# New orders of the steps in the attention loops of a four-layer transformer on one core

## The chip, the cores and the metric

The kernel runs on one core of a Trainium2 chip. The metric is the device time of one execution in microseconds. The core has five engines that each work through a queue of their own, strictly in the order in which the program put the instructions: TensorE (PE), VectorE (DVE), ScalarE (ACT), GpSimd (POOL) and SyncE (SP, here for DMAs alone). They meet only through semaphores.

## What is computed

Eight sequences of 256 tokens, width 128, pass through four layers. Each layer is a gated cross attention on a context of 64 tokens and a gated feed-forward block (mixtures of experts in layers 0, 1 and 3, a plain gated one in layer 2). Cut to the attention:

```
x = x + tanh(g_xattn[L]) * attn_L(layernorm(x), ctx)     # x: (8, 256, 128), ctx: (8, 64, 128)
x = x + tanh(g_ffn[L])   * ffn_L(layernorm(x))           # for L = 0..3

attn_0, attn_2:  16 heads of 8, keys and values from ctx; attn_2 adds a mask before the softmax
attn_1:          16 heads of 8, keys and values from ctx and from x itself (64 + 256 keys),
                 the first key gets tanh(gate), a layernorm follows before the output projection
attn_3:          8 heads of 64, keys and values from ctx
```

## The kernel before

Everything stays in SBUF; the program is a row of stages (`setup`, then attention and feed-forward of each layer, then `store`). The change lies in `attention` (layers 0, 1, 2) and `attention3` (layer 3).

An attention stage has a prologue (weights split into high and low parts, the keys of all sequences) and a loop over the eight sequences b. The work of one sequence is cut into steps, for 16-head layers by group g of four heads (g = 0 to 3), in layer 1 also by the set of keys i (i = 0 the context's, i = 1 to 4 one head's own). On the engines, a step is this:

- `scale` (DVE L804, layer 3 L1181): normalises x into `xn`. `turn`: PE transposes `xn` (L518, L1035), ACT and DVE split the result into `xt_hi` and `xt_lo` (L686, L810), POOL adds the output bias to x (L394, L987).
- `proj` (g): PE multiplies with the weights (L535 to L537) into the one bank `b_proj`; ACT takes a part (L698), DVE makes `q` from the bank and the part (L823). PE's next `proj` waits for that (`qk_split`), since the bank is the same. In layer 3 the two `proj` (L1044 to L1046) are copied by ACT (L1137).
- `keys` (g): POOL spreads this sequence's keys into `kc` (L398). It waits until the last sequence's `weights` of this group have read it.
- `scores` (g): PE multiplies `q` and `kc` (L551, mask L553; own keys L558; layer 3 L1057); it waits for `q` and `kc`. DVE reduces to a maximum (L835, L837, L1192) and puts it in `mx` (L847, L849, L1197).
- `maxima` (g): PE transposes the maxima (L571, L1064), ACT and DVE split them (L705, L858, L860; layer 3 L1142, L1203).
- `weights` (g): PE computes the scores again, transposed and less their maximum (L586, L588, L590, L591, L597, layer 3 L1073 and L1074); ACT takes the exponential (L711, L1147).
- `values` and `spread`: POOL lays out the values (L405, L1008), and in layer 1 those of x itself. `pv`: PE multiplies with them (L624, L1092), ACT copies the result (L725). Layer 3 also has `sums` (PE L1081, DVE reciprocal L1208), `parts` (ACT L1152, DVE L1213) and `divide` (PE L1100, ACT copy L1157, DVE L1220).
- `o_turn`, `o_norm`, `o_scale`, `on_turn`, `y`: the result is transposed back (L641), divided (L865, L868), in layer 1 normalised (POOL L465, DVE L888), transposed (L647), projected (L653, L1114) and added to x (L895, L1226).
- `mask_in`, `mask` (layer 2): POOL copies this sequence's mask (L458), PE transposes it (L526), ACT and DVE split it (L692, L817), POOL keeps a copy (L453). `scores` waits for the DVE's part.

The order of the steps is written out by hand in one table for each layer, `STEPS_0` to `STEPS_3`. An entry names a step, an offset to the pass number v, and the group. Each engine goes over the same table and issues its own part of each step, so a table sets the order of four queues at once:

```
def passes(eng, does):
    for v in range(-2, B + 3):
        for step, db, *at in table:
            if step in does and 0 <= v + db < B:
                does[step](v + db, *at)
```

Work of up to three sequences is so interleaved. The offset and the place in the table together say how far a step stands behind another. Every wait is inside its step and moves with it.

Of the kernel before, what the change touches and what calls it, by code (L numbers as in the profile page):

```python
# [113 lines left out]
def setup(pr):  # L114
# [2176 lines left out]
```

## Time and profile before

| | us |
|---|---|
| median of 3 runs | 1176.37 |
| the three runs | 1165.46, 1176.37, 1176.54 |
| the profiled execution | 1168.41 |
| its span (first to last instruction) | 1166.6 |

| loop over the eight sequences | first `scale` starts | last `y` on DVE starts |
|---|---|---|
| layer 0 | 35.6 | 125.6 |
| layer 1 | 208.2 | 442.2 |
| layer 2 | 747.5 | 861.8 |
| layer 3 | 943.7 | 1069.7 |

Over the whole span PE is busy for 78%, DVE 64%, ACT 48%, POOL 37%; but these are means over stages with different limits, so the loops are read one by one. A matmul's time in the profile runs to its modelled end, while the next may start some 0.12 us after it; PE's idle time is therefore read from starts.

### The profile page before, as it was taken

What the parts mean: (1) busy time and instruction counts of PE and PEld (TensorE: products, weight loads), DVE (VectorE), ACT (ScalarE), POOL (GpSimd) and SP (SyncE); (2) the same over time, 40 slices, a digit from 0 to 9 for tenths busy, and PEclk for the clock granted to TensorE, in tenths of its full rate; (3) what the DMA queues carried; (4) which work ended last, traced back from release to release, by engine and by line L of the source; (5) the groups of instructions that cost most, each with busy time, mean ns of one, the idle gap of its engine ahead of it and who ended that gap; (6) DMA issues with size and microseconds to landing.
All of it is one profiled execution on the core that took longest, in us unless ns stands there. A gap on an engine that the chain in (4) does not pass through costs nothing. (4 is left out here: it accounts for less than half of the span.)

```text
span 1166.6 us, 17099 instructions
## 1 busy us (share of the span) xinstructions
PE 912.0 (78%) x5366; PEld 686.6 (59%) x5366; DVE 746.8 (64%) x1823; ACT 563.8 (48%) x1091; POOL 428.7 (37%) x575
## 2 busy tenths in 40 slices
PE   2799586689899885888888885688858588885696
PEld 2677464556565643666666663477745357884574
DVE  3688467579998865757666564467756414555576
ACT  0477253367776762545555543256634233331364
POOL 2333414133443323655656565233310132220434
PEclk9799688689998995999999998689979769998699
DMA  4000000000001000000000001000000200000001
GB/s 129 1 2 2 1 0 22 1 20 20 19 21 37 20 2 0 1 1 1 1 1 1 1 1 23 16 2 1 2 21 1 72 1 1 1 1 1 0 1 37
DMA packets 25606, 14.12 MB, mean 12 GB/s; under 512 B 10775, under 2 KB 25006, under 8 KB 25390
## 3 DMA queue, kind: packets, MB, share of 16 engines
q1 hardware_dynamic: 25518, 13.03, 4.2%
q8 instruction: 45, 0.74, 0.3%
q14 instruction: 43, 0.35, 0.1%
HBM read 11.98 MB, written 1.05 MB: 11 GB/s over the span
## 5 line engine op out<-in xcount | busy, mean ns | idle before, releaser
L1433 POOL TENSOR_TENSOR L1f_h<-L1f_h,L1f_gb 128x512 f32<-128x512 f32 (+1 forms) x96 | 152.2, 1589 | 105.5 <-DVE L1f_h L1726 97.3
L711 ACT ACTIVATE L_pt<-bank 128x512 f32<-128x512 f32 x224 | 127.1, 597 | 44.0 <-PE bank L597 35.0
L398 POOL TENSOR_TENSOR L_kc<-L_kc_all,const 128x256 fp32r<-128x256 f32 x96 | 59.1, 618 | 177.8 <-PE bank L597 114.1
L698 ACT ACTIVATE L_part<-bank,L_bias_ca,const 128x256 fp32r<-128x256 f32 x128 | 68.9, 563 | 89.3 <-PE bank L537 88.8
L1562 ACT ACTIVATE L1f_a<-bank 128x512 f32<-128x512 f32 (+1 forms) x96 | 57.3, 597 | 112.7 <-PE bank L1487 112.6
L1726 DVE TENSOR_TENSOR L1f_h<-L1f_a,bank 128x512 f32<-128x512 f32 (+1 forms) x96 | 65.5, 682 | 70.8 <-ACT L1f_a L1562 70.3
L1734 DVE TENSOR_TENSOR L1f_h_lo<-L1f_h,L1f_h_hi 128x512 fp32r<-128x512 f32 (+1 forms) x96 | 88.2, 919 | 11.1 <-ACT L1f_h_hi L1575 11.1
L837 DVE TENSOR_REDUCE L_ms<-bank 128x2 f32<-128x512 f32 x128 | 84.0, 686 | 7.3 <-PE bank L558 7.2
L835 DVE TENSOR_REDUCE L_mc<-bank 128x8 f32<-128x512 f32 (+1 forms) x96 | 65.4, 682 | 19.5 <-PE bank L553 12.2
L1485 PE MATMUL bank<-L1f_xt_hi,big_hi 128*128 128x512 f32 (+1 forms) x192 | 77.8, 405 | 0.0
L1486 PE MATMUL bank<-L1f_xt_lo,big_hi 128*128 128x512 f32 (+1 forms) x192 | 76.8, 400 | 0.0
L1487 PE MATMUL bank<-L1f_xt_hi,big_lo 128*128 128x512 f32 (+1 forms) x192 | 76.7, 400 | 0.0
L558 PE MATMUL bank<-L_k,L_q 32*128 32x256 f32 x256 | 54.3, 335 | 16.6 <-DVE L_ms L837 15.1
L551 PE MATMUL bank<-L_kc,L_q 128*128 128x256 f32 x192 | 54.1, 345 | 15.8 <-DVE L_msk L817 6.4
L1507 PE MATMUL bank<-L1f_h_hi,big_hi 128*128 128x512 f32 (+1 forms) x96 | 41.4, 431 | 30.0 <-DVE L1f_h_lo L1734 29.7
L823 DVE SCALAR_TENSOR_TENSOR L_q<-bank,L_bias_c,L_part 128x256 fp32r<-128x256 f32 x96 | 46.2, 482 | 25.8 <-ACT L_part L698 23.6
L1575 ACT CAST L1f_h_hi<-L1f_h 128x512 fp32r<-128x512 f32 (+1 forms) x96 | 59.0, 615 | 2.1 <-POOL L1f_h L1433 2.1
L558 PEld LDWEIGHTS bank<-L_k,L_q 32*128 32x128 f32 x256 | 35.5, 199 | 32.9 <-DVE L_ms L837 21.3
L535 PE MATMUL bank<-L_xt_hi,L_wx 128*128 128x256 f32 x128 | 43.1, 337 | 9.9 <-DVE L_xt_lo L810 9.9
L551 PEld LDWEIGHTS bank<-L_kc,L_q 128*128 128x128 f32 x192 | 34.5, 208 | 27.6 <-issue 16.5
L705 ACT ACTIVATE L_hm<-bank,const 128x256 fp32r<-128x256 f32 x96 | 45.1, 470 | 6.3 <-PE bank L571 6.1
L1507 PEld LDWEIGHTS bank<-L1f_h_hi,big_hi 128*128 128x128 f32 (+1 forms) x96 | 17.9, 187 | 49.9 <-DVE L1f_h_lo L1734 44.8
(412 smaller groups left out, 2570.2 us busy)
## 6 DMA issues: line engine op xcount, KB each, us to landing
L_raw<-in_L_ffn_w_dram SPq DMA_DIRECT2D x8, 176.0 KB, 2.3
L_raw<-in_L_ffn_v_dram SPq DMA_DIRECT2D x8, 176.0 KB, 2.4
const<-in_const_dram SPq DMA_DIRECT2D x1, 1036.0 KB, 5.1
x<-in_x_dram SPq DMA_DIRECT2D x2, 512.0 KB
L_raw<-in_L_ffn_w_dram SPq DMA_DIRECT2D x8, 128.0 KB, 2.5
L_mask<-in_mask_Bx1xSxS_ff_dram SPq DMA_DIRECT2D x2, 512.0 KB
out_dram<-x SPq DMA_DIRECT2D x2, 512.0 KB
L_raw<-in_L_ffn_w_dram SPq DMA_DIRECT2D x8, 48.0 KB, 2.6
```

The source lines that it names most:

```text
L551: last = pe.matmul(o[:, t * S:(t + 1) * S], q[:, g, ts], kc[:, g], start=True, stop=not masked)
L558: last = pe.matmul(o[:, t * S:(t + 1) * S], q[rows, g, t * P:(t + 1) * P], k[rows, g], start=True, stop=True)
L698: last = act.activation(part[:, i].bitcast(F32R), b_proj[:, i * S:(i + 1) * S], ACT.Identity, bias=bias_ca[:, i, g:g + 1], scale=pr.c("ak" ...
L711: act.activation(pt[:, g // 2, (g % 2) * NS + (HEADS_1[i] if own_keys else i)], b_st[(g * NS + i) % 2][:], ACT.Exp, scale=scale).then_inc( ...
L835: dve.tensor_reduce(mc[:].rearrange("p t j -> p (t j)"), by_head[:, :, start:], AX_X, ALU.max).then_inc(sem["sc_taken"], 1)
L837: dve.tensor_reduce(ms[:, :, i - 1], bank.rearrange("p (t s) -> p t s", s=S), AX_X, ALU.max).then_inc(sem["sc_taken"], 1)
L1433: pool.tensor_tensor(h[0:m, r], h[0:m, r], gb[0:m, gate_slot(c)], ALU.mult).then_inc(sem["h_done"], 1)
L1485: pe.matmul(bank[0:m], hi[:, at:at + m], xh, start=True, stop=False)
L1486: pe.matmul(bank[0:m], hi[:, at:at + m], xl, start=False, stop=False)
L1487: last = pe.matmul(bank[0:m], lo[:, at:at + m], xh, start=False, stop=True)
L1726: dve.tensor_tensor(h[0:m, r], a[0:m, r], b_u[c % NS][0:m], ALU.mult).then_inc(sem["half_done"], 1)
L1734: dve.tensor_tensor(h_lo[0:m, r], h[0:m, r], h_hi[0:m, r].bitcast(F32), ALU.subtract).then_inc(sem["lo_done"], 1)
```

## The change

The four tables are replaced. The steps in each are the same ones, the bodies of the steps, their waits, the buffers and the prologues of the stages as well; what changes is the place and the offset of the entries, and so the order in the queues of PE, DVE, ACT and POOL. No DMA moves.

For layers 0 and 2, this is PE's queue over one turn of the loop. Digits are the groups, b is the sequence whose `turn` begins the row.

```
layer 0 before: turn(b) scores3(b-1) proj0(b) maxima2(b-1) weights1(b-1) o_turn(b-2) scores0(b) proj1(b)
  maxima3(b-1) weights2(b-1) pv0(b-1) on_turn(b-2) scores1(b) proj2(b) maxima0(b) weights3(b-1) y(b-2)
  scores2(b) proj3(b) maxima1(b) weights0(b) pv1(b-1)
layer 0 after:  turn(b) maxima1(b-1) weights0(b-1) scores3(b-1) pv1(b-2) proj0(b) maxima2(b-1)
  weights1(b-1) o_turn(b-2) proj1(b) maxima3(b-1) weights2(b-1) on_turn(b-2) scores0(b) proj2(b)
  pv0(b-1) scores1(b) y(b-2) maxima0(b) proj3(b) weights3(b-1) scores2(b)
layer 2 before: as layer 0 before, with mask(b) between weights1(b-1) and o_turn(b-2)
layer 2 after:  turn(b) weights0(b-1) scores3(b-1) maxima2(b-1) proj0(b) weights1(b-1) o_turn(b-2)
  mask(b) proj1(b) weights2(b-1) scores0(b) maxima3(b-1) on_turn(b-2) proj2(b) scores1(b) pv0(b-1)
  maxima0(b) weights3(b-1) y(b-2) scores2(b) proj3(b) maxima1(b) pv1(b-1)
layer 3 before: turn(b) pv0(b-1) sums(b-1) proj0(b) y(b-2) proj1(b) scores0(b) scores1(b) pv1(b-1)
  maxima(b) divide0(b-1) divide1(b-1) weights0(b) weights1(b)
layer 3 after:  turn(b) divide1(b-2) weights0(b-1) proj0(b) weights1(b-1) proj1(b) pv0(b-1) sums(b-1)
  scores0(b) scores1(b) y(b-2) maxima(b) divide0(b-1) pv1(b-1)
```

On POOL, `keys` moves against `turn` in all layers (in layer 1, `turn(b)` now stands ahead of `keys0(b)`); on DVE, `scale(b+1)` moves ahead, in layer 2 from behind `y(b-2)` to behind `proj1(b)`, in layer 0 to behind `maxima2(b-1)`. In layer 1 a few entries swap with their neighbours.

```diff
--- before.py
+++ after.py
@@ -172,40 +172,40 @@
 
 
 STEPS_0 = (
-    ("values", 0), ("scale", 1), ("scores", 0, 2, 0), ("proj", 0, 3), ("keys", 0, 3), ("maxima", 0, 1), ("weights", 0, 0, 0), ("pv", -1, 1, 0),
-    ("turn", 1), ("scores", 0, 3, 0), ("proj", 1, 0), ("keys", 1, 0), ("maxima", 0, 2), ("weights", 0, 1, 0), ("spread", 0), ("o_turn", -1),
-    ("o_norm", -1), ("scores", 1, 0, 0), ("proj", 1, 1), ("keys", 1, 1), ("maxima", 0, 3), ("weights", 0, 2, 0), ("pv", 0, 0, 0), ("o_scale", -1),
-    ("on_turn", -1), ("scores", 1, 1, 0), ("proj", 1, 2), ("keys", 1, 2), ("maxima", 1, 0), ("weights", 0, 3, 0), ("y", -1),
+    ("keys", 0, 0), ("o_scale", -2), ("weights", -1, 3, 0), ("scores", 0, 2, 0), ("turn", 1), ("maxima", 0, 1), ("weights", 0, 0, 0),
+    ("scores", 0, 3, 0), ("pv", -1, 1, 0), ("proj", 1, 0), ("keys", 0, 1), ("maxima", 0, 2), ("keys", 0, 2), ("weights", 0, 1, 0), ("scale", 2),
+    ("o_turn", -1), ("o_norm", -1), ("proj", 1, 1), ("keys", 0, 3), ("maxima", 0, 3), ("weights", 0, 2, 0), ("on_turn", -1), ("scores", 1, 0, 0),
+    ("proj", 1, 2), ("pv", 0, 0, 0), ("scores", 1, 1, 0), ("y", -1), ("maxima", 1, 0), ("proj", 1, 3), ("spread", 0), ("values", 1),
 )
 
 STEPS_1 = (
-    ("y", -2), ("weights", -1, 3, 3), ("keys", 0, 2), ("keys", 0, 3), ("weights", -1, 3, 4), ("scores", 0, 1, 4), ("scores", 0, 2, 0), ("scale", 1),
-    ("proj", 0, 3), ("values", 0), ("maxima", 0, 1), ("pv", -1, 1, 0), ("weights", 0, 0, 0), ("pv", -1, 1, 1), ("keys", 1, 0), ("scores", 0, 2, 1),
-    ("scores", 0, 2, 2), ("weights", 0, 0, 1), ("weights", 0, 0, 2), ("pv", -1, 1, 2), ("weights", 0, 0, 3), ("scores", 0, 2, 3),
-    ("weights", 0, 0, 4), ("scores", 0, 2, 4), ("turn", 1), ("weights", 0, 1, 0), ("scores", 0, 3, 0), ("scores", 0, 3, 1), ("maxima", 0, 2),
-    ("proj", 1, 0), ("spread", 0), ("pv", -1, 1, 3), ("pv", -1, 1, 4), ("scores", 0, 3, 2), ("weights", 0, 1, 1), ("weights", 0, 1, 2),
-    ("scores", 0, 3, 3), ("scores", 0, 3, 4), ("o_turn", -1), ("weights", 0, 1, 3), ("weights", 0, 1, 4), ("o_norm", -1), ("scores", 1, 0, 0),
-    ("proj", 1, 1), ("weights", 0, 2, 0), ("pv", 0, 0, 0), ("weights", 0, 2, 1), ("weights", 0, 2, 2), ("scores", 1, 0, 1), ("scores", 1, 0, 2),
-    ("maxima", 0, 3), ("pv", 0, 0, 1), ("pv", 0, 0, 2), ("weights", 0, 2, 3), ("scores", 1, 0, 3), ("o_scale", -1), ("weights", 0, 2, 4),
-    ("scores", 1, 0, 4), ("proj", 1, 2), ("keys", 1, 1), ("on_turn", -1), ("scores", 1, 1, 0), ("maxima", 1, 0), ("weights", 0, 3, 0),
-    ("pv", 0, 0, 3), ("pv", 0, 0, 4), ("scores", 1, 1, 1), ("weights", 0, 3, 1), ("weights", 0, 3, 2), ("scores", 1, 1, 2), ("scores", 1, 1, 3),
+    ("y", -2), ("weights", -1, 3, 3), ("weights", -1, 3, 4), ("scores", 0, 1, 4), ("scores", 0, 2, 0), ("scale", 1), ("proj", 0, 3), ("values", 0),
+    ("maxima", 0, 1), ("weights", 0, 0, 0), ("scores", 0, 2, 1), ("scores", 0, 2, 2), ("pv", -1, 1, 0), ("pv", -1, 1, 1), ("weights", 0, 0, 1),
+    ("weights", 0, 0, 2), ("pv", -1, 1, 2), ("weights", 0, 0, 3), ("scores", 0, 2, 3), ("weights", 0, 0, 4), ("scores", 0, 2, 4), ("turn", 1),
+    ("weights", 0, 1, 0), ("scores", 0, 3, 0), ("scores", 0, 3, 1), ("maxima", 0, 2), ("proj", 1, 0), ("scores", 0, 3, 2), ("pv", -1, 1, 3),
+    ("pv", -1, 1, 4), ("scores", 0, 3, 3), ("weights", 0, 1, 1), ("weights", 0, 1, 2), ("keys", 1, 0), ("spread", 0), ("scores", 0, 3, 4),
+    ("o_turn", -1), ("o_norm", -1), ("weights", 0, 1, 3), ("weights", 0, 1, 4), ("scores", 1, 0, 0), ("proj", 1, 1), ("weights", 0, 2, 0),
+    ("pv", 0, 0, 0), ("keys", 1, 1), ("weights", 0, 2, 1), ("weights", 0, 2, 2), ("scores", 1, 0, 1), ("scores", 1, 0, 2), ("maxima", 0, 3),
+    ("pv", 0, 0, 1), ("pv", 0, 0, 2), ("keys", 1, 2), ("weights", 0, 2, 3), ("weights", 0, 2, 4), ("o_scale", -1), ("scores", 1, 0, 3),
+    ("scores", 1, 0, 4), ("proj", 1, 2), ("weights", 0, 3, 0), ("scores", 1, 1, 0), ("maxima", 1, 0), ("scores", 1, 1, 1), ("keys", 1, 3),
+    ("pv", 0, 0, 3), ("pv", 0, 0, 4), ("on_turn", -1), ("weights", 0, 3, 1), ("weights", 0, 3, 2), ("scores", 1, 1, 2), ("scores", 1, 1, 3),
 )
 
 HEADS_1 = (0, 2, 3, 4, 1)
 VALUES_AFTER_1 = (1, 5, 5, 4, 4)
 
 STEPS_2 = (
-    ("values", 0), ("scale", 1), ("mask_in", 1), ("scores", 0, 2, 0), ("proj", 0, 3), ("keys", 0, 3), ("maxima", 0, 1), ("weights", 0, 0, 0),
-    ("pv", -1, 1, 0), ("turn", 1), ("scores", 0, 3, 0), ("proj", 1, 0), ("keys", 1, 0), ("maxima", 0, 2), ("weights", 0, 1, 0), ("spread", 0),
-    ("mask", 1), ("o_turn", -1), ("o_norm", -1), ("scores", 1, 0, 0), ("proj", 1, 1), ("keys", 1, 1), ("maxima", 0, 3), ("weights", 0, 2, 0),
-    ("pv", 0, 0, 0), ("o_scale", -1), ("on_turn", -1), ("scores", 1, 1, 0), ("proj", 1, 2), ("keys", 1, 2), ("maxima", 1, 0), ("weights", 0, 3, 0),
-    ("y", -1),
+    ("spread", 0), ("turn", 1), ("o_scale", -2), ("weights", 0, 0, 0), ("scores", 0, 3, 0), ("maxima", 0, 2), ("proj", 1, 0), ("o_norm", -1),
+    ("weights", 0, 1, 0), ("o_turn", -1), ("mask", 1), ("proj", 1, 1), ("keys", 1, 3), ("scale", 2), ("weights", 0, 2, 0), ("scores", 1, 0, 0),
+    ("maxima", 0, 3), ("on_turn", -1), ("proj", 1, 2), ("scores", 1, 1, 0), ("pv", 0, 0, 0), ("maxima", 1, 0), ("weights", 0, 3, 0), ("y", -1),
+    ("values", 1), ("scores", 1, 2, 0), ("proj", 1, 3), ("maxima", 1, 1), ("keys", 2, 0), ("mask_in", 2), ("keys", 2, 1), ("keys", 2, 2),
+    ("pv", 0, 1, 0),
 )
 
 STEPS_3 = (
-    ("values", 0), ("scale", 1), ("weights", 0, 0), ("weights", 0, 1), ("turn", 1), ("pv", 0, 0), ("sums", 0), ("proj", 1, 0), ("keys", 1, 0),
-    ("y", -1), ("proj", 1, 1), ("keys", 1, 1), ("parts", 0), ("scores", 1, 0), ("scores", 1, 1), ("pv", 0, 1), ("maxima", 1), ("divide", 0, 0),
-    ("divide", 0, 1),
+    ("divide", -1, 0), ("pv", -1, 1), ("turn", 1), ("scale", 2), ("divide", -1, 1), ("weights", 0, 0), ("proj", 1, 0), ("weights", 0, 1),
+    ("values", 1), ("proj", 1, 1), ("pv", 0, 0), ("sums", 0), ("scores", 1, 0), ("scores", 1, 1), ("parts", 0), ("y", -1), ("keys", 2, 0),
+    ("keys", 2, 1), ("maxima", 1),
 )
 
 
```

## Rows read from the trace of the kernel before

**Rows 1.** The page's first line.
```profile
span 1166.6 us, 17099 instructions
```

**Rows 2.** Windows: one sequence's turn in layers 0, 1, 1 again, 2, 3; PEclk is the granted clock.
```profile
core 0: us, PE busy (x) PEld busy (x) DVE busy (x) ACT busy (x) POOL busy (x), PEclk, DMA share, GB/s
76.70:86.20 9.50, 8.88 (x74) 7.00 (x73) 8.27 (x23) 6.84 (x16) 3.68 (x7) 1.00 0.01 3
...
283.90:309.40 25.50, 22.72 (x210) 14.95 (x208) 24.34 (x55) 18.68 (x40) 9.86 (x21) 1.00 0.08 22
...
360.40:387.30 26.90, 24.82 (x203) 16.11 (x203) 23.72 (x54) 17.98 (x38) 9.94 (x21) 0.84 0.07 22
...
799.10:811.70 12.60, 10.80 (x92) 9.11 (x92) 9.02 (x25) 7.89 (x17) 4.43 (x9) 1.00 0.01 1
...
1015.40:1029.20 13.80, 12.28 (x83) 10.92 (x82) 6.88 (x14) 4.47 (x9) 3.35 (x7) 1.00 0.00 1
```

**Rows 3.** Timeline, layer 0: start, length, engine, line; one group's steps on PE, ACT, DVE.
```profile
81.39 0.48 PE L551 MATMUL bank<-L_kc,L_q 128*128 128x256 f32 x2
81.71 0.28 PE L535 MATMUL bank<-L_xt_hi,L_wx 128*128 128x256 f32 x1
...
82.07 0.38 PE L571 MATMUL bank<-const,L_mx 128*128 128x128 f32 x2
82.20 0.36 PE L588 MATMUL bank<-L_q,L_kc 128*128 128x256 f32 x1
...
82.85 0.64 PE L624 MATMUL bank<-L_pt,L_vc 128*32 128x256 f32 x8
83.42 0.44 PE L647 MATMUL bank<-const,L_on 128*128 128x128 f32 x2
83.64 0.48 PE L551 MATMUL bank<-L_kc,L_q 128*128 128x256 f32 x2
...
82.27 0.57 ACT L698 ACTIVATE L_part<-bank,L_bias_ca,const 128x256 fp32r<-128x256 f32 x1 [0.64 <-PE bank L537]
...
83.06 0.48 DVE L823 SCALAR_TENSOR_TENSOR L_q<-bank,L_bias_c,L_part 128x256 fp32r<-128x256 f32 x1
```

**Rows 4.** Timeline, POOL and DVE at once, layers 0 and 1.
```profile
50.08 1.16 DVE L849 COPY L_mx<-L_mc 128x16 f32<-128x16 f32 x1
...
288.66 0.73 POOL L394 TENSOR_TENSOR x<-x,L_bo 128x256 f32<-128x256 f32 x1
...
288.92 0.50 DVE L847 TENSOR_TENSOR L_mx<-L_mc,L_ms 128x16 f32<-128x16 f32 x1
```

**Rows 5.** Timeline of PE, layer 2: the three places where it stands.
```profile
802.34 0.38 PE L535 MATMUL bank<-L_xt_hi,L_wx 128*128 128x256 f32 x1 [0.45 <-DVE L_xt_lo L810]
...
803.61 0.28 PE L591 MATMUL bank<-L_mt,L_selc 128*128 128x256 f32 x1
804.55 0.41 PE L526 MATMUL bank<-const,L_mk 128*128 128x128 f32 x2 [0.67 <-DVE L_mt L860]
804.80 0.60 PE L641 MATMUL bank<-const,L_ot 128*128 128x128 f32 x4
806.08 0.36 PE L551 MATMUL bank<-L_kc,L_q 128*128 128x256 f32 x1 [0.68 <-DVE L_msk L817]
```

**Rows 6.** Timeline, layer 3: PE before its stands, and the DVE's reciprocal.
```profile
1008.57 0.28 PE L1046 MATMUL bank<-L_xt_hi,L_wq_lo 128*128 128x256 f32 x1
1009.58 2.05 PE L1057 MATMUL bank<-L_kb,L_q 128*128 128x128 f32 x16 [0.73 <-ACT L_q L1137]
...
1014.20 0.67 PE L1073 MATMUL bank<-L_q,L_kb 128*128 128x256 f32 x2 [0.66 <-ACT L_rb L1157]
...
1005.68 1.76 DVE L1208 RECIPROCAL L_rs<-bank 128x256 f32<-128x256 f32 x1 [1.44 <-PE bank L1081]
```

**Rows 7.** Windows: early sequences of layers 0 and 2.
```profile
45.60:57.20 11.60, 10.52 (x55) 9.15 (x56) 8.66 (x20) 6.51 (x14) 7.25 (x11) 0.61 0.01 1
...
747.50:786.50 39.00, 30.15 (x190) 25.50 (x191) 22.37 (x55) 19.14 (x39) 12.99 (x26) 0.74 0.00 1
```

## The prediction

> **What bounds the kernel now.** I read the page's first line for the span [rows 1], then windows of one sequence's turn in the steady part of each loop [rows 2], then the timeline of each engine inside such a turn [rows 3, 5, 6]. The windows are to show which engine is nearly always at work; the timelines which wait ends last. The turns take 9.5 us (layer 0), 25.5 (layer 1), 12.6 (layer 2) and 13.8 (layer 3), and five or six of the eight are alike. Layer 1 is DVE's: 24.34 of 25.50 us busy, so little is to be had by any order. In layer 0 DVE is busy for 8.27 of 9.50. In layers 2 and 3 DVE has much room (9.02 of 12.60, 6.88 of 13.80), and PE, which looks full, is not: its busy time runs to the matmuls' modelled ends, 0.16 us past the point where the next could start. By starts, PE stands still where its queue comes to a step whose data are on their way through ACT and DVE. The loops are bound by the order of waits.
>
> **Layer 0, one turn.** The old order puts `scores` of a group just ahead of the next `proj`, and `scores` needs the `q` of the `proj` before. So each group is one closed chain: `scores` 0.32 us on PE (81.39 to 81.71), `proj` to ACT 0.56 (to 82.27), ACT to DVE about 0.6 when nothing is in the way, DVE 0.48, and 0.1 to PE: 2.1 to 2.2 us, and 2.25 here (81.39 to 83.64) [rows 3]. Three such and 3.1 us around `turn` make 9.5. The new order puts `scores` one group later. Then `proj` waits for its own bank alone: 0.56 + 0.6 + 0.48 + 0.1 = 1.75, with the first matmul after a wait somewhat longer 1.85. I walked the new table with these durations. `proj0` to `proj1`: 1.85. `proj1` to `proj2`: 2.10, since on DVE `maxima2`, the moved `scale`, and `o_norm` now stand ahead of the part of `proj1`. `proj2` to `proj3`: 1.85. `proj3` to the next `proj0`: PE itself is full, with `proj` 0.36, `maxima` 0.13, `weights` 0.57 (0.65 here with a short wait at its end), `pv` 0.57, `scores` 0.32 [rows 3]: one `proj`, two `weights`, two `scores`, one `pv`, one `maxima` and about 0.3 for `turn` are 3.14. Sum 8.94, so 0.6 less per turn; five steady turns give 3.0. The first two turns run at the half clock [rows 7] and have the same chains with longer matmuls, the last has an end of its own; I take 1.8 for the three. **Layer 0: 4.8.**
>
> **Layer 2, one turn.** PE stands three times. Before `proj0`, 0.45 + 0.16, for `xt_lo`. Before `mask`, from 803.61 + 0.12 to 804.55, 0.82, since `mask` shares a bank with `maxima2`, which DVE has only just read. Before `scores0`, from about 805.24 (four transposes, 0.11 each, after 804.80) to 806.08, 0.84, for the mask's way over ACT and DVE [rows 5]. Together 2.3; without them PE's queue is 10.3 to 10.5 us long. In the new order `weights0`, `scores3` and `maxima2`, some 1.5 us, lie between `turn` and `proj0` and cover the first; `proj0`, `weights1` and `o_turn` between `maxima2` and `mask`, some 1.4, cover the second; `proj1` and `weights2`, 1.25, between `mask` and `scores0` cover the third. Walked through with DVE and ACT, no stand over 0.1 us is left: 10.55.
>
> One cost comes back. DVE instructions that read and write SBUF alone take longer when one of POOL runs: the copy into `mx`, 0.18 us otherwise, took 1.16 beside POOL's split, and the one of layer 1 0.50 beside L394 [rows 4]. In the walk `scale` now falls on POOL's `keys2` and `spread`, and the copy after `scores0` on POOL's x + bias. What `scale` loses beside POOL in a steady turn no row here shows; from below nothing, from above the 0.98 us that the copy lost beside the split. I take 0.45, nearer to the copy beside L394, and it reaches PE at `maxima0`: 11.0, 1.6 less per turn. The Trainium skill ("SBUF — State Buffer", Who interferes with whom) says the port pair that the two engines share is an exclusive lock for a whole instruction; by that rule both instructions of `scale` could wait for one POOL instruction each, and the layer would get about 2 us less. Five steady turns: 8.0. In the first turns PE stands at every group for `q` or the mask (30.15 busy in 39.0 [rows 7]); walked, `proj0` of sequence 2 comes 3 us earlier. The end gives 1. **Layer 2: 12.**
>
> **Layer 3, one turn.** PE stands before `scores0` from 1008.69 to 1009.58, 0.89, for ACT's copy of `q`; before `maxima`, 0.3; and from about 1013.4 to 1014.20, 0.8, for ACT's copies in `divide` [rows 6]: 2.0 of 13.8. The new order puts `pv0` and `sums` (2.4 us) between `proj1` and `scores0`, `turn` and `weights0` between the halves of `divide`, and the other `weights` half between the two `proj`. All three stands are covered. What comes next is DVE: `sums` now ends just ahead of `scores`, its reciprocal of 1.76 us [rows 6] starts at 7.3 us in the turn, the two reductions and the copy follow to 10.65, and `maxima` stands behind `y` at 10.7: no more than 0.05 late; `divide0` then waits 0.15 for `parts`. With 0.1 for the extra changes between number formats the turn is 12.3: 1.5 less. Counted from `weights` to `weights` six turns are steady: 9.0, and 0.7 at the end. **Layer 3: 9.7.**
>
> **Layer 1, one turn.** DVE idles 1.2 of 25.5 us, and half of that are the short gaps between dependent instructions. The one thing that changes is that POOL does L394 ahead of `keys0`, which stands until `weights0` is done. So L394 no longer falls on the copy L847: 0.50 against 0.18 [rows 4], 0.3 saved on the bounding engine, and 0.1 by `scores` moved ahead of `pv`. Bounds: nothing and 0.7. 0.4 times seven. **Layer 1: 3.**
>
> **The sum.** 4.8 + 3 + 12 + 9.7 = 29.5 us. The profiled execution took 1168.4 (span 1166.6 [rows 1], 1.8 around it), so 1138.9 for one like it. The runs of before are 1165.5, 1176.4 and 1176.5; with the profiled one their mean is 1171.7. I forecast a time like that mean: 1171.7 - 29.5 = 1142.
>
> **The rivals.**
> *Half of it* (1157): in layers 2 and 3 a new wait takes the place of each old one. For it: `pv0` of layer 2 comes only 0.4 us after POOL's `spread` in my walk, and POOL's queue (`keys`, `mask_in`, `spread`, x + bias, `mask`) is strict; a late `keys2` would hold PE. Against: POOL is busy for 4.43 of 12.60 us [rows 2]. Price: 0.8 us in 16 turns, 13 to 15 us back.
> *More* (1131): PE's clock comes back to full sooner in the first turns. PE ran at 0.61 of full there, mostly at 1.2 GHz and not 2.4 [rows 7], with PE waiting between groups; the new order waits less. If 5 us less in each of three layers are at the half clock, about half of PE's time in it comes back, 2.5 each, 7.5 in all, and the lock in layer 2 may cost nothing, 3. The Trainium skill ("TensorE: Matmul & The Clock Gate", Part 1) says that activity releases the throttle, which would do just that. But the fall to 0.84 in layer 1 came in a turn like its neighbours and cost 1.4 us (26.90 against 25.50) [rows 2], so some of it is chance.
> *No change* (1170): the four tables only move the same stands elsewhere, since the sum of the chain per group stays. Against: the chain of layer 0 loses a member, and in layers 2 and 3 real work lies under each stand.
> *Slower* (1190): `proj` issued ahead of `scores` stands in PE's strict queue until DVE has read the bank, and `scores`, which could have fed DVE, stands behind it; DVE starves and is later still for the next. Place: `proj1` to `proj3` in layers 0 and 2, 48 in all. It decides where each is 29.5 / 48 = 0.6 us later than in the old order; with 1.0, a reduction of DVE and part of another instruction ahead of it, it costs 48 and gives 1171.7 - 29.5 + 48 = 1190. The walk has DVE late at one of these (by 0.35), so I give it little.
>
> **The numbers.** My sum 0.62, half of it 0.17, more 0.10, no change 0.07, slower 0.04. The range that leaves out the last two and the ends of the others is 1128 to 1161. Faster by over 1% than 1176.4 (below 1164.6; 1% is about what a measurement of this kernel can tell from no change, its own runs being 11 us apart) are the first three but for a slice of the second: 0.86. Within 1%: 0.09. Slower: 0.05.
>
> **What would show it.** Right: turns of about 8.9, 25.1, 11.0 and 12.3 us; `proj` to `proj` 1.85 in layer 0; no wait of PE for `L_msk` or for L860 before L526; in layer 3 no wait for `L_q` or `L_rb` above 0.2; L847 at 0.18 all through. The lock: L804 in layer 2 longer than 0.34 with POOL beside it. Wrong: PE waiting for L823 ahead of L535 for over 0.4 in each group, PE waiting for POOL's L398 or L405, or layer 1 slower than 25.5. The layers I am least sure of are 2, where the lock may take 0 to 0.9 per turn, and the first turns of each loop.

## The result, and the profile after

| | before | after |
|---|---|---|
| median | 1175.14 us (6 runs, 1165.46 to 1176.54) | 1123.07 us (6 runs, 1116.40 to 1132.88) |
| ratio, 95% interval | | 0.958 [0.9546, 0.9615] |
| profiled execution, span | 1168.41, 1166.6 | 1132.88, 1131.1 |

The change is faster by 52 us at the medians. Forecast were 1142 us and a gain of 29.5, so 1123 lies below the range of 1128 to 1161. The profiled execution of after is the slowest of its six, as that of before was among the fast ones, so these two profiles alone show a gain of only 35.5. A second profile of the same kernel, further down, took 1117.63.

First the page's line and the windows of one turn in layers 0, 1, 2 and 3, which answer to [rows 1] and [rows 2], and the stretch that ends layer 1's loop:

```profile
span 1131.1 us, 17100 instructions
```

```profile
core 0: us, PE busy (x) PEld busy (x) DVE busy (x) ACT busy (x) POOL busy (x), PEclk, DMA share, GB/s
82.50:91.40 8.90, 8.58 (x75) 7.02 (x74) 8.59 (x23) 7.13 (x17) 3.62 (x7) 1.00 0.00 0
260.00:284.70 24.70, 23.04 (x211) 15.59 (x210) 23.50 (x54) 18.43 (x39) 9.85 (x22) 1.00 0.08 24
384.20:442.70 58.50, 50.41 (x366) 30.30 (x365) 35.13 (x83) 30.00 (x61) 16.21 (x38) 0.73 0.04 11
798.50:808.80 10.30, 10.30 (x92) 8.98 (x92) 9.12 (x23) 7.89 (x18) 4.33 (x10) 1.00 0.01 2
986.00:997.50 11.50, 11.50 (x83) 10.83 (x81) 6.51 (x12) 4.68 (x9) 3.39 (x7) 1.00 0.01 1
```

In layers 2 and 3 PE is now busy for the whole turn. The timeline of PE in layer 2, where [rows 5] showed stands of 0.45, 0.67 and 0.68 us, has the same lines and no idle time before any of them:

```profile
801.49 0.38 PE L571 MATMUL bank<-const,L_mx 128*128 128x128 f32 x2
801.63 0.36 PE L535 MATMUL bank<-L_xt_hi,L_wx 128*128 128x256 f32 x1
...
802.77 0.60 PE L641 MATMUL bank<-const,L_ot 128*128 128x128 f32 x4
803.21 0.38 PE L526 MATMUL bank<-const,L_mk 128*128 128x128 f32 x2
803.51 0.36 PE L535 MATMUL bank<-L_xt_hi,L_wx 128*128 128x256 f32 x1
804.71 0.35 PE L551 MATMUL bank<-L_kc,L_q 128*128 128x256 f32 x1
```

The next table takes all profiles of this study, sorted by which table of steps the layer had. A loop runs from its first `scale` to the end of its last `y`; the turn is the median distance of two `y` in the steady part.

| | old table: loop, mean (lowest to highest), turn | new table | gain | forecast |
|---|---|---|---|---|
| layer 0 | 91.2 (90.2 to 92.2), 9.53, 9 profiles | 85.1 (84.3 to 86.6), 8.86, 9 | 6.1 | 4.8 |
| layer 1 | 241.8 (234.5 to 247.7), 25.5 to 27.3, 7 | 231.9 (227.4 to 239.6), 24.70, 6 | 9.9 | 3 |
| layer 2 | 114.7 (114.2 to 115.6), 12.57, 9 | 96.3 (95.8 to 97.3), 10.30, 9 | 18.4 | 12 |
| layer 3 | 125.0 (123.2 to 126.5), 13.80, 10 | 109.5 (108.1 to 110.7), 11.57, 9 | 15.5 | 9.7 |

These are 49.9 of the 52 us. Layer 1 is the one whose loop differs from profile to profile: the profile of before has the shortest old one (234.5), that of after the longest new one (239.6). This explains why the two profiles differ by so much less than the medians.

### The profile page after: what moved, and what is told of

It reads as the page before. It is cut to its first block and busy times, and to the rows that moved or that the text cites. A ratio compares the mean times of both kernels' runs of the same rounds, so it can differ in the third digit from the quotient of the medians.

```text
span 1131.1 us, 17100 instructions
## 1 busy us (share of the span) xinstructions
PE 910.0 (80%) x5366; PEld 688.7 (61%) x5366; DVE 743.6 (66%) x1823; ACT 566.2 (50%) x1091; POOL 427.3 (38%) x575
## 5 line engine op out<-in xcount | busy, mean ns | idle before, releaser
L558 PE MATMUL bank<-L_k,L_q 32*128 32x256 f32 x256 | 57.1, 346 | 9.1 <-DVE L_ms L837 7.8
L823 DVE SCALAR_TENSOR_TENSOR L_q<-bank,L_bias_c,L_part 128x256 fp32r<-128x256 f32 x96 | 46.2, 482 | 24.9 <-ACT L_part L698 23.0
L551 PE MATMUL bank<-L_kc,L_q 128*128 128x256 f32 x192 | 49.9, 323 | 4.3 <-DVE L_k L823 2.0
L535 PE MATMUL bank<-L_xt_hi,L_wx 128*128 128x256 f32 x128 | 45.8, 358 | 8.8 <-DVE L_q L823 4.7
L558 PEld LDWEIGHTS bank<-L_k,L_q 32*128 32x128 f32 x256 | 37.0, 205 | 21.6 <-DVE L_ms L837 12.3
L597 PE MATMUL bank<-L_mt,L_k 32*128 32x256 f32 x256 | 45.0, 351 | 2.4 <-ACT L_pt L711 1.4
```

The costliest lines, as they stand in the source:

```text
L558: last = pe.matmul(o[:, t * S:(t + 1) * S], q[rows, g, t * P:(t + 1) * P], k[rows, g], start=True, stop=True)
```

## Experiments

**Each table alone.** Four kernels, each the old one with one new table, and the new one with layer 1's old table:

```diff
-STEPS_0 = (("values", 0), ("scale", 1), ...)      # likewise STEPS_1, STEPS_2, STEPS_3
+STEPS_0 = (("keys", 0, 0), ("o_scale", -2), ...)
```

> The new table of layer 0 alone. Theory A (each loop gains by itself, the sizes in the forecast were off): loop 90.5 to 86.0 us, turn 9.53 to 8.85, the whole 4 to 5 us shorter. Theory B (the tables help one another through the clock of the stages that follow): less than 3 us, or a change in the stages behind the loop.

> The new table of layer 1 alone. Theory A: turns of 24.7 us in place of 25.5 where the clock is full, the loop 5 to 7 us shorter in an execution whose clock is alike; the profiled execution of the changed kernel had its loop at 239.6 because 41 us at its end ran at the half clock, and most executions are not like it. Theory C (the new table itself makes PE fall to the half clock more often): the median is no better than before, the loop is above 234 in most executions.

> The new table of layer 2 alone. Theory A: turn 12.57 to 10.3, loop 114.8 to about 96.5, the whole 18 us shorter. Theory B: 12 or less, as forecast at first.

> The new table of layer 3 alone. Theory A: turn 13.80 to 11.57, loop 126.5 to about 111, the whole 15 to 16 us shorter. Theory B: 10 or less.

> The new tables of layers 0, 2 and 3, the old one of layer 1. Theory A (the tables add up): the sum of the three alone, 3.7 + 18.2 + 21.5, would be 43 us, by the loops of the profiles 5 + 18.5 + 15 = 38 us, so a median of 1133 to 1138. If layer 1's new table gives 12 us more at the median, this kernel is that much slower than the changed one. Theory D (layer 1's table is worth its shorter turns only, 3 to 6 us): it is within 6 us of the changed kernel's 1123.

| new table in | median, us | ratio, 95% interval | its loop in the profile |
|---|---|---|---|
| layer 0 | 1172.10 (before, here and in the next three rows, 1175.78) | 0.9985 [0.9951, 1.0019] | 84.9 |
| layer 1 | 1163.26 | 0.9893 [0.9825, 0.9961] | 228.3 |
| layer 2 | 1157.54 | 0.9843 [0.9783, 0.9904] | 95.8 |
| layer 3 | 1154.23 | 0.9820 [0.9755, 0.9885] | 109.7 |
| 0, 2 and 3 | 1137.09 (before 1174.17) | 0.9676 [0.9635, 0.9718] | layer 1 (old): 247.7 |

The four gains are 3.7, 12.5, 18.2 and 21.5 us, together 56 against 52 for the whole. As far as intervals of up to 8 us to each side can tell, they add up and no layer's table spoils another. Layer 3's 21.5 is 6 us more than its loop gives; with four runs the interval reaches from 13 to 29, so the loop's 15.5 is the better figure. Layer 1's is 12.5 alone and 14.0 on top of the others (1137.1 against 1123.1), where 3 were forecast. Layer 0 alone cannot be told from no change by its time; its loop is 5.6 us shorter than in the profile of before. In its profiled execution the old layer 1 loop took 246.8, which hides that; whether it did so in the other nine is not on record.

**Layer 2: one wait at a time, and the price of POOL beside DVE.**

```diff
 # l2_scores0_only: old kernel, STEPS_2
-("scores", 1, 0, 0), ("proj", 1, 1), ("keys", 1, 1), ("maxima", 0, 3), ("weights", 0, 2, 0),
+("proj", 1, 1), ("keys", 1, 1), ("maxima", 0, 3), ("weights", 0, 2, 0), ("scores", 1, 0, 0),
 # l2_scale_late: new kernel, STEPS_2
-("keys", 1, 3), ("scale", 2), ("weights", 0, 2, 0), ... ("y", -1),
+("keys", 1, 3), ("weights", 0, 2, 0), ... ("y", -1), ("scale", 2),
```

> The old tables; in layer 2 only scores0 goes behind weights2, past the stand for the mask (0.84 us). If the stands come off one by one, the turn goes from 12.57 to 11.7 to 12.0. If another stand takes its place (q of group 1, or the other two stands grow), it stays at 12.3 or more.

> The changed kernel, in layer 2 scale(b+1) back behind y(b-2). Forecast's view: scale no longer beside POOL's keys and spread, so 0.34 us an instruction and the turn no longer, or shorter by up to 0.2. Rival: POOL's x + bias waits for scale, and mask and keys3 stand behind it in POOL's queue, so that PE's weights0 waits for mask: turn 10.3 to 10.8 or more.

`l2_scores0_only` took 1166.78 us in its one run; the turn went from 12.57 to 12.17, between the two expectations, and the loop from 114.8 to 111.4. The waits of PE in four turns of the loop, first of before, then of this kernel (in total, times, longest):

```profile
PE bank L551 <- DVE L_msk L817: 2.7, 4, 0.7
PE bank L526 <- DVE L_mt L860: 2.7, 4, 0.7
PE bank L535 <- DVE L_xt_lo L810: 1.8, 4, 0.5
```

```profile
PE bank L526 <- DVE L_mt L860: 2.7, 4, 0.7
PE bank L535 <- DVE L_xt_lo L810: 1.8, 4, 0.5
PE bank L571 <- DVE L_msk L817: 1.3, 4, 0.3
```

The wait for the mask goes from L551, 0.68 a turn, to the next `maxima`, 0.33 a turn: `proj1`, `maxima3` and `weights2` are work that fits under it, but `maxima3` shares a bank that the mask's reader holds. Only the new table, which puts `maxima3` behind `scores0`, clears it: the same view of after has no line at all in this stretch, and none in layer 3's.

`l2_scale_late` puts `scale` where POOL is idle. The groups of both instructions over the whole loop, of after and then of this kernel (busy us, mean ns of one | idle before):

```profile
L849 DVE COPY L_mx<-L_mc 128x16 f32<-128x16 f32 x32 | 6.5, 203 | 1.1
L804 DVE TENSOR_SCALAR L_xn<-x,L_mv,L_rstd 128x128 f32<-128x128 f32 x16 | 5.5, 381 | 0.0
```

```profile
L849 DVE COPY L_mx<-L_mc 128x16 f32<-128x16 f32 x32 | 8.3, 258 | 1.1
L804 DVE TENSOR_SCALAR L_xn<-x,L_mv,L_rstd 128x128 f32<-128x128 f32 x16 | 5.0, 355 | 0.0
```

In each steady turn of after, the first of the two instructions of `scale` takes 0.46 us and the second 0.34. With `scale` late both take 0.34, but the copy beside L394 then takes 0.55 and not 0.26. So `scale` beside POOL costs DVE 0.12 us a turn, and both kernels have a turn of 10.30: the 0.45 us that the prediction added isn't there. DVE is busy for 9.12 of 10.30, so it would also have room for it. The Trainium skill ("SBUF — State Buffer", Who interferes with whom) says that the second of two such instructions blocks until the first ends. The trace agrees: `keys2` (0.62 us on POOL) starts 0.25 us ahead of `scale`, and `scale` ends 0.08 us behind it; the copy beside L394 ends 0.03 us behind that one in both kernels. What is paid is what is left of POOL's instruction, not the whole of it.

**Layer 3: where `y` stands.**

```diff
 # l3_y_early: new kernel, STEPS_3
-("proj", 1, 0), ("weights", 0, 1), ... ("parts", 0), ("y", -1), ("keys", 2, 0),
+("proj", 1, 0), ("y", -1), ("weights", 0, 1), ... ("parts", 0), ("keys", 2, 0),
```

> The changed kernel, in layer 3 y back behind proj0. If y covers DVE's reciprocal, PE now stands before maxima for about 1.6 us and the turn is 12.8 to 13.2 in place of 11.57. If the reciprocal isn't in the way, it stays below 11.8.

One run of 1130.94 us; the layer's turn is 13.61 and no longer 11.57, the loop 124.8. That is more than the 12.8 to 13.2 that were expected. Most of it is one wait, 1.4 of the 2.0 us a turn, here in some five turns:

```profile
PE bank L1064 <- DVE L_mx L1197: 7.1, 5, 1.4
```

The long queue of DVE (reciprocal 1.76, two reductions, the copy) needs PE work behind `scores`; `y`, 1.8 us, is that work. So layer 3's gain is not a matter of removed stands alone: what is put under DVE's new chain is worth 2.0 us a turn.

**Layer 0: one distance or the whole table.**

```diff
 # l0_scores_first: new kernel, STEPS_0, each scores back ahead of the proj that follows
-("scores", 0, 2, 0), ("turn", 1), ... ("proj", 1, 1), ... ("scores", 1, 0, 0), ("proj", 1, 2), ("pv", 0, 0, 0), ("scores", 1, 1, 0),
+("turn", 1), ... ("scores", 1, 0, 0), ("proj", 1, 1), ... ("scores", 1, 1, 0), ("proj", 1, 2), ("pv", 0, 0, 0), ... ("scores", 1, 2, 0),
 # l0_scores_later: old kernel, STEPS_0, only these three scores put behind the next proj
-("scores", 1, 0, 0), ("proj", 1, 1), ... ("scores", 1, 1, 0), ("proj", 1, 2),
+("proj", 1, 1), ... ("scores", 1, 0, 0), ("proj", 1, 2), ("scores", 1, 1, 0),
```

> The changed kernel; in layer 0 scores of groups 0, 1 and 2 back ahead of the next proj. If the closed chain scores, proj, ACT, DVE is what bound the old order, the turn goes from 8.86 back to 9.3 to 9.6 us. If the gain came from turn, maxima and scale being earlier, it stays below 9.1.

> The old tables; in layer 0 scores of groups 0, 1, 2 behind the next proj, nothing else. If the closed chain of scores and proj is the bound, the turn goes from 9.53 to 8.9 to 9.1. If it takes the earlier scale, turn and maxima too, it stays above 9.2.

Both are slower than either kernel's own table: 10.61 us a turn for the first, 10.34 for the second, against 8.86 and 9.53 (one run each, 1143.27 and 1177.42 us). In the first, `scores1` and `proj2` behind it stand for `q`, whose DVE part has `o_norm`, a reduction and a copy ahead of it:

```profile
96.10 0.47 PE L551 MATMUL bank<-L_kc,L_q 128*128 128x256 f32 x2 [1.26 <-DVE L_q L823]
```

In the second `maxima` comes right behind the late `scores`, and PE waits for the copy that was just started (waits from 75 to 112 us); its wait ahead of `proj0` is also longer, 0.8 us and not 0.5:

```profile
PE bank L571 <- DVE L_mx L849: 1.6, 4, 0.4
```

So the one idea of the prediction, `scores` a group later, is no gain by itself, and the rest of the new table is none without it. In the new table `maxima` and `weights` move too, by about a group, so that PE has work while DVE reduces.

**Layer 1: first the obvious causes.** Forecast was that `keys0` moves and L394 no longer falls on L847.

```diff
 # l1_keys_only: old kernel, STEPS_1
-("pv", -1, 1, 1), ("keys", 1, 0), ("scores", 0, 2, 1), ... ("turn", 1),
+("pv", -1, 1, 1), ("scores", 0, 2, 1), ... ("turn", 1), ("keys", 1, 0),
 # l1_swap_only: old kernel, STEPS_1
-("pv", -1, 1, 3), ("pv", -1, 1, 4), ("scores", 0, 3, 2),
+("scores", 0, 3, 2), ("pv", -1, 1, 3), ("pv", -1, 1, 4),
 # l1_both: both of these.  new_unswapped_1: new kernel with the swap undone
```

> The old tables, with keys of group 0 of the next sequence behind turn in layer 1, as in the new one; only POOL's queue changes. If the copy beside POOL's x + bias was the cost: L847 back to 0.18 us, the turn 25.5 to 25.2. Else the turn stays at 25.5 and the new table's 24.7 has other causes.

> The old tables; in layer 1 scores3 of key set 2 goes ahead of pv of the sequence two back, the one swap of the new table that fills the stretch in which PE's stand ended most often just before the clock fell. Theory E (that stand of 0.95 us, behind L837, makes PE fall to the half clock): the steady turns stay at a granted clock of 0.98 or more, the loop is 232 or less, the median 5 us or more below the kernel before. Theory F (the clock keeps up because of the length of the turn, 24.7 in place of 25.5, or for all swaps together): the turns stay between 25.4 and 27.3 with a clock of 0.82 to 1.

> The old tables; in layer 1 both the swap of scores3 (key set 2) ahead of pv and keys of group 0 behind turn on POOL. If what shortens the turn is DVE's instructions beside POOL's, and the two moves together are what the new table does to them: turn at full clock 24.7 (24.95 with the swap alone), L847 near 0.22 us on average. If the clock follows from a turn that short: turns 3 to 7 at 0.99 or more in four of five, loop 228 to 232, median 8 to 12 us below before. If the clock has another cause in the new table, it goes on falling and the median is 5 to 7 below.

> The changed kernel with this one swap undone in layer 1. Theory E: half-clock stretches come back in the steady turns, the loop goes to 236 or more in most executions, the median to 1128 or more. Theory F: turns stay at 24.7 to 24.9 and 1.00, median within 3 us of 1123.

Measured: `l1_keys_only` 1172.39 us, ratio 0.9992 [0.9960, 1.0024]; `l1_swap_only` 1169.78, 0.9981 [0.9951, 1.0011]; `l1_both` 1171.23, 0.9971 [0.9951, 0.9992]; `new_unswapped_1` 1127.20, 0.9627 [0.9587, 0.9667]. The times decide little: the three old kernels are 2 to 5 us below before, and the interval of `new_unswapped_1` overlaps that of the changed kernel. The profiles say more. `l1_keys_only` keeps turns of 25.4 to 27.0. In `l1_swap_only` turns of 24.9 and 26.5 us alternate, which fits neither theory. `l1_both` has 24.8 at the full clock, and the clock goes on falling. `new_unswapped_1` has its half-clock stretches back and a loop of 240.7, as theory E says.

What DVE gains is there, in three turns each, before and then after:

```profile
L847 DVE TENSOR_TENSOR L_mx<-L_mc,L_ms 128x16 f32<-128x16 f32 x12 | 4.6, 387 | 0.4
L873 DVE TENSOR_TENSOR L_o<-L_on,L_vg_all 128x256 bf16<-128x256 f32 x3 | 2.1, 694 | 0.1
L888 DVE TENSOR_SCALAR L_on<-L_o,L_mvb,L_rstdb 128x128 f32<-128x128 bf16 x6 | 1.8, 339 | 0.0
```

```profile
L847 DVE TENSOR_TENSOR L_mx<-L_mc,L_ms 128x16 f32<-128x16 f32 x12 | 2.6, 221 | 0.4
L888 DVE TENSOR_SCALAR L_on<-L_o,L_mvb,L_rstdb 128x128 f32<-128x128 bf16 x6 | 2.3, 420 | 0.0
L873 DVE TENSOR_TENSOR L_o<-L_on,L_vg_all 128x256 bf16<-128x256 f32 x3 | 1.6, 524 | 0.1
```

L847 loses 0.67 us a turn, L873 0.17, L888 gains 0.16: together 0.7 of the 0.8 by which a turn at full clock is shorter (25.5 to 24.7). These means hide that most of it is one event. In 25 of 35 old turns (turns 3 to 7 of the seven profiles with the old table), L847 or L873, some 7 us into the turn, is caught behind (starts right after and ends only with) one of POOL's L446, the split of the next stage's weights, and takes 0.95 us and not 0.18, or 1.23 and not 0.42. The first three rows are of before; the last two of `l0_scores_later`, with the same table of layer 1, where DVE isn't caught:

```profile
320.13 2.74 POOL L446 TENSOR_TENSOR big_lo<-L_raw,big_hi 128x352 fp32r<-128x352 f32 x3
320.14 0.95 DVE L847 TENSOR_TENSOR L_mx<-L_mc,L_ms 128x16 f32<-128x16 f32 x1
321.86 0.42 DVE L873 TENSOR_TENSOR L_o<-L_on,L_vg_all 128x256 bf16<-128x256 f32 x1
...
357.27 2.85 POOL L446 TENSOR_TENSOR big_lo<-L_raw,big_hi 128x352 fp32r<-128x352 f32 x3
357.28 0.18 DVE L847 TENSOR_TENSOR L_mx<-L_mc,L_ms 128x16 f32<-128x16 f32 x1
```

An old turn at the full clock takes 25.5 us when it is caught (five turns) and 24.71 when not (the one in `l0_scores_later`), as long as a new one. None of the 30 new turns is caught. It is the swap that does it: none of five turns in `l1_swap_only` and in `l1_both`, five of five in `new_unswapped_1`, four of five in `l1_keys_only`.

What is left over is the clock. Windows ahead of such a fall and in it, in before:

```profile
314.00:320.70 6.70, 5.71 (x51) 3.81 (x50) 6.46 (x13) 4.37 (x11) 4.12 (x13) 1.00 0.00 0
320.80:324.20 3.40, 3.40 (x25) 2.37 (x23) 3.17 (x11) 2.23 (x6) 3.32 (x6) 0.51 0.00 0
```

The long stand of PE in those 6.7 us ends some 2 us ahead of the fall to 1.2 GHz, on the timeline:

```profile
318.87 0.51 PE L558 MATMUL bank<-L_k,L_q 32*128 32x256 f32 x2 [0.95 <-DVE L_ms L837]
```

In the kernel with the swap and the keys this stand is 0.53 us and not 0.95, but another one, 17 us into the turn, is followed by a fall in every other turn. Its line on the timeline:

```profile
306.63 0.50 PE L558 MATMUL bank<-L_k,L_q 32*128 32x256 f32 x2 [0.55 <-DVE L_ms L837]
```

Windows of this kernel, the 6 us up to that fall and the stretch in it:

```profile
302.50:308.50 6.00, 4.90 (x45) 3.37 (x46) 5.71 (x14) 4.15 (x9) 0.17 (x1) 1.00 0.01 4
308.70:312.00 3.30, 3.30 (x22) 2.63 (x20) 2.51 (x7) 2.34 (x6) 0.96 (x2) 0.50 0.02 5
```

**Layer 1: the second place.** This made the last theory, that the old table reaches the half clock through two places of its turn, and that each has its own entry.

```diff
 # new_pv_early_1: new kernel, STEPS_1, two pv back ahead of the scores
-("weights", 0, 0, 0), ("scores", 0, 2, 1), ("scores", 0, 2, 2), ("pv", -1, 1, 0), ("pv", -1, 1, 1),
+("pv", -1, 1, 0), ("weights", 0, 0, 0), ("pv", -1, 1, 1), ("scores", 0, 2, 1), ("scores", 0, 2, 2),
 # l1_three: l1_both and this.  new_tail_1: new kernel with the like of it undone
-("on_turn", -1), ("scores", 1, 1, 0), ("maxima", 1, 0), ("weights", 0, 3, 0), ("pv", 0, 0, 3), ("pv", 0, 0, 4), ("scores", 1, 1, 1),
+("weights", 0, 3, 0), ("scores", 1, 1, 0), ("maxima", 1, 0), ("scores", 1, 1, 1), ("pv", 0, 0, 3), ("pv", 0, 0, 4), ("on_turn", -1),
```

> The changed kernel; in layer 1 pv of key sets 0 and 1 (second half of the heads) back ahead of scores2 of sets 1 and 2, the other swap. If this swap keeps the clock up: half-clock stretches in the steady turns, median 1127 or more. If it does nothing: turn 24.7 at 1.00, median 1119 to 1126.

> The old kernel; in layer 1 alone three edits: keys0 of the next sequence behind its turn, scores(3, own head 2) ahead of two pv, and now on_turn behind pv(0, 3 and 4), with weights(3, context) ahead of scores(1, context) and scores(1, 1) ahead of the two pv, as the new table has them. With the first two edits alone PE still fell to the half clock in every other full turn, 2.0 us after a step of 0.82 us between two matmul starts (L558, waiting for L837), 19 us into the turn. Theory: the half clock is reached through two places of the turn, this one and the old one of 1.21 us at 4.9 us; the first is mended by the swap, the second by on_turn's new place. Then no step above 0.7 us is left behind L647, layer 1 runs turns of 24.7 to 24.9 us without half clock from turn 3 on, its loop is 228 to 231 us, and the kernel takes 1162 to 1165 us, like the new table alone (1163.3). Rival: it is the places of keys 1 to 3 or pv(1, 0) that do it; then the half clock still comes in every other turn (26.4 us), the loop is 234 to 237, and the time 1170 to 1172.

> The new kernel; in layer 1 on_turn goes back ahead of scores(1, context), weights(3, context) behind maxima, and scores(1, 1) behind the two pv. Theory (two places of the turn lead to the half clock): the step of about 0.8 us between two matmul starts comes back 17 us into the turn, with it the half clock in every other turn (26.4 us), loop 233 to 237 and not 229.6, kernel 1128 to 1131 us. Rival (it is another entry): full clock stays, loop 229 to 232, kernel 1122 to 1125.

> The changed kernel once more, for its own spread and one more profile. If the profile shown at first (layer 1's loop 239.6 us, 0.85) was an outlier of the clock, layer 1's loop is 227 to 232 here and the median stays at 1120 to 1126.

Medians: `new_pv_early_1` 1124.08, ratio 0.9579 [0.9543, 0.9616]; `l1_three` 1165.57, 0.9943 [0.9909, 0.9976]; `new_tail_1` 1131.81, 0.9660 [0.9608, 0.9712]; `changed_again` 1122.78, 0.9568 [0.9531, 0.9604]. The time of turns 3 to 7 of layer 1 together, and how far into a turn the falls to the half clock began (counted from about 0.6 us behind the first matmul of `turn`), in each profile; each kernel with an edit has one profile, so five turns:

| layer 1's table | turns 3 to 7, us | falls at, us into the turn |
|---|---|---|
| old, 7 profiles | 129.2 to 136.2 | 6 to 7 and 18 to 21, 4 to 9 of them |
| old + keys | 131.6 | 6.8, 19.0, 19.5, 6.2, 19.9, 6.5 |
| old + swap | 128.3 | 6.8, 18.9, 18.6 |
| old + both | 127.8 | 6.6, 18.8, 18.8 |
| old + both + tail | 124.1 | 6.6 |
| new - tail | 127.2 | 18.9, 18.9 |
| new - swap | 129.7 | 5.9, 6.3, 6.9, 20.7 |
| new - pv | 124.9 | 6.8 |
| new, 6 profiles | 123.5 to 124.9 | none (3), 6.6 (1), 6.8 (1), 6.4 and 6.7 (1) |

The swap takes away most of the falls early in the turn: there are 27 in the 45 turns of all kernels without it, 8 in the 55 with it. The tail takes away those late in it: 29 in 55 turns without it, 1 in 45 with it. Both hold in both directions, from the old table and from the new. The two kinds don't cost the same. A late fall makes a turn 1.4 to 1.6 us longer, and DVE idles for 2.5 us in it and not 1.1; an early one makes it 0.6 to 0.8 longer, and 0.1 to 0.3 where DVE is caught behind L446 as well. With all three edits the old table has the new one's steady turns (124.1), its 24.70 us turn and its loop (227.9 us, the new table alone had 228.3). Its median, 1165.6, stands 2 us above that of the new table alone. Against the before that was measured with each, the gains are 7.6 and 12.5 us; the two intervals overlap, so the times do not show that the three edits give all of it. One of the twelve executions of `l1_three` took 4257 us, and nothing on record explains it; the median of the others is 1165.0. `new_pv_early_1` changed next to nothing (turns of 24.8, one fall), and `new_tail_1` came out as its theory said (loop 236.8, with 1131.8 us just above the 1128 to 1131).

The far end of what a table can do to the clock is in `t0_alone`, whose old layer 1 fell twice in every turn. Two of its turns:

```profile
282.00:309.30 27.30, 25.14 (x210) 16.95 (x212) 24.49 (x54) 18.60 (x39) 9.82 (x21) 0.87 0.08 21
309.30:336.60 27.30, 25.15 (x210) 16.98 (x212) 24.52 (x54) 18.63 (x39) 9.84 (x21) 0.87 0.07 21
```

DVE has as much to do there as in [rows 2] (24.5 us), the turn is 1.8 longer. The second profile of after, in contrast, kept the full clock over the five turns; one of them:

```profile
253.30:278.00 24.70, 23.02 (x210) 15.57 (x209) 23.53 (x53) 18.47 (x38) 9.86 (x21) 1.00 0.08 24
```

No kernel here beats the changed one: `changed_again`, `new_pv_early_1` and `l2_scale_late` (1120.4, one run) are all within its range.

## Why the prediction missed

The direction, the layers and their mechanism were right; it was the size, 52 us where 29.5 stood, in three of four terms. The step with the largest miss is layer 1's, that no order could gain much on DVE; then come the first turns and POOL's price in layer 2, and the durations in layer 3. By its own steps:

**What bounds the kernel.** Right for layers 0, 2 and 3. For layer 1 the step "DVE is busy for 24.34 of 25.50, so little is to be had by any order" failed. It read a turn at the full clock, and 25.50 is not what a turn costs: the old table's turns 3 to 7 average 26.4 (131.9 by five over seven profiles), the new one's 24.8. The row with 26.90 at 0.84 [rows 2] was there, and the prediction put it down to chance. It is the order of the steps: 6 of 35 such old turns were at the full clock throughout, and 26 of 30 new ones.

**Layer 0, 4.8: right.** 8.94 forecast, 8.86 measured; the loop gives 6.1, 3.4 in five turns (3.0 forecast) and 2.7 in the others (1.8). `proj` to `proj` by the starts of L535 is 1.89, 1.99, 1.98 and 2.99 (1.85, 2.10, 1.85 and 3.14 forecast):

```profile
84.97 0.39 PE L535 MATMUL bank<-L_xt_hi,L_wx 128*128 128x256 f32 x1
...
86.86 0.36 PE L535 MATMUL bank<-L_xt_hi,L_wx 128*128 128x256 f32 x1
...
88.85 0.32 PE L535 MATMUL bank<-L_xt_hi,L_wx 128*128 128x256 f32 x1
...
90.83 0.36 PE L535 MATMUL bank<-L_xt_hi,L_wx 128*128 128x256 f32 x1
...
93.82 0.39 PE L535 MATMUL bank<-L_xt_hi,L_wx 128*128 128x256 f32 x1
```

The walk through four queues held; the short form of it, "`scores` one group later", would not have, as the two edits show.

**Layer 2, 12: mechanism right, 6.4 us too small.** All three stands are gone. The turn is 10.30, not 11.0: the cost that "comes back" did not, and PE's queue is 10.3 long, at the low end of the 10.3 to 10.5 that the prediction named. Over five turns that is 11.3 where 8.0 stood. The first `y` starts 30.8 us into the loop and not 38.6, so 7.8 sooner, where 3 were taken for the first turns. The end lost 0.6 where 1 was to be gained. In the window of the first turns the granted clock is 0.85 and was 0.74 [rows 7]:

```profile
747.10:778.30 31.20, 26.83 (x196) 22.75 (x196) 22.07 (x58) 19.91 (x40) 12.45 (x25) 0.85 0.00 1
```

But the clock doesn't explain the 7.8. Up to the first `y` it lies between 0.70 and 0.80 in the nine profiles of the old table, and `y` comes at 38.6 to 39.9; in the nine of the new one between 0.78 and 0.85, and `y` comes at 30.7 to 31.5. At 0.80 it is 38.6 and 31.5. So it was the waits of the first turns that were priced too low, and of the rival "more" only the part on POOL's price was right for this layer.

**Layer 3, 9.7: mechanism right, 5.8 too small.** The turn is 11.57, not 12.3. The chain that should have set it is there, and sooner. From the start of `turn` at 987.09, `sums` lets the reciprocal start after 6.9 us (7.3 forecast), and `maxima` follows at 10.2 (10.7):

```profile
987.09 0.38 PE L1035 MATMUL bank<-const,L_xn 128*128 128x128 f32 x2
...
992.03 1.89 PE L1081 MATMUL bank<-L_pt,const 128*128 128x256 f32 x8
993.75 1.95 PE L1057 MATMUL bank<-L_kb,L_q 128*128 128x128 f32 x16
995.54 1.95 PE L1114 MATMUL bank<-L_wo,L_on 128*128 128x128 f32 x16
997.33 0.38 PE L1064 MATMUL bank<-const,L_mx 128*128 128x128 f32 x2
...
993.96 1.76 DVE L1208 RECIPROCAL L_rs<-bank 128x256 f32<-128x256 f32 x1 [4.50 <-PE bank L1081]
```

The rows of before gave longer durations. `scores` is 1.79 from start to start here (993.75 to 995.54) and 1.89 there, behind a stand; the two halves of `proj` are 0.71 each here, right behind `weights`, and 0.90 and 0.80 there, behind `sums` and `y`. The prediction's 0.1 for changes between formats was on top. Removed stands were worth 2.0 and the shorter steps about 0.2; no loss came back, where 0.5 had been put. Five turns gave 10.9 us and what follows them 5.3; 0.7 was lost ahead of the first `y`. Forecast were 9.0 and 0.7 for six turns and the end.

**Layer 1, 3: failed.** L847 beside L394: the sign and the size were right (0.50 to 0.18), but it was not "the one thing that changes". The larger cost was DVE caught behind L446, 0.8 us in 25 of 35 turns, which the prediction didn't see, though its upper bound of 0.7 a turn is near it. The gaps between DVE instructions, which the prediction took for untouchable, stayed at 1.1 to 1.2 us in a turn at the full clock. The falls of the clock were put at nothing. Over the 35 old and 30 new turns, DVE is busy for 24.30 and 23.65 us on average and idle for 2.08 and 1.15: of 1.58 us a turn, 0.65 is shorter work and 0.93 are waits that come with the falls. Forecast was 0.4.

**The base.** The forecast was made for a run of 1171.7 while the median of before is 1175.1. This made the error 3.4 smaller than that of the gain.

**The rivals.** "More" had the nearest time (1131), mostly by luck: of its two reasons, that POOL might cost layer 2 nothing held (3 us); the clock of the first turns isn't what shortened layer 2; and what layers 1 and 3 gave beyond the sum is in neither. "Half of it", "no change" and "slower" did not come: PE never waits for POOL in layer 2, and in layer 0's steady turns it has no wait for L823 of over 0.4 (in the first turns up to 1.3). An order can be slower, though: `l0_scores_later`, three entries moved alone, loses 0.8 us a turn. But PE waits for L823 nowhere in its steady turns; the loss is at `maxima` and ahead of `proj0`, not where "slower" looked.

## What to carry to other kernels

Where one table sets the order of several queues, walk all the queues, and put work under each new chain before you count a removed wait: the same idea in three entries cost 0.8 us a turn, in the whole table it gave 0.7. Take step durations from rows that stand in the same surroundings as in the new order. Price DVE beside POOL by what is left of POOL's instruction when DVE's starts, and look at the longest instance of each instruction of the bounding engine, not at its mean. Where an engine that isn't PE bounds a loop, read the granted clock over several turns, too, before you say that the order of PE's steps is worth nothing.

## What was not expected of the hardware

The order of PE's work changed how often the clock fell in a loop that DVE bounds: 41 falls in 35 turns of the old table, 4 in 30 of the new. In layer 1 two stands of PE, each 0.5 to 1 us long at a fixed place of the turn, were followed 1 to 2.3 us later by a fall to the half clock, in some turns or in every one, and a loop that fell at both places ran turns of 27.3 instead of 25.5 us. A stand's length doesn't tell by itself: in `l1_three` PE stands 0.79 us for L847 in each turn, and no fall follows it.

```profile
303.20 0.44 PE L571 MATMUL bank<-const,L_mx 128*128 128x128 f32 x2 [0.79 <-DVE L_mx L847]
```

The Trainium skill ("TensorE: Matmul & The Clock Gate", HAM oscillation — how this bites in real kernels) tells of a loop that falls to the half clock in every pass, by waits of 3 to 5 us. Here far shorter stands are followed by falls. What exactly the chip adds up is not settled by these runs.
